# A hybrid of deformable convolution, attention and experts on one core: where the image is added after the sampling, and where TensorE's branch stands

## What is computed

```python
x = x + deform_conv2d(_gn(x), offset_w, offset_b, weight, bias)
x = x + self_attention(_gn(x), ...)            # 1024 x 1024 scores
t = _to_tokens(x)
t = t + attention(_ln_t(t), ...)               # with a fixed bias by distance
t = t + experts(_ln_t(t), ...)                 # top 2 of 8 experts
t = t + linear_attention(_ln_t(t), ...)        # 16 heads of 8
t = t + experts(_ln_t(t), ...)
x = _from_tokens(t, x)
```

## Time and profile before

| | |
|---|---|
| median of three runs | 2330.2 us |
| the profiled execution's own time | 2326.0 us |
| its span, first to last instruction | 2324.2 us |
| TensorE busy, of the span | 81% |
| VectorE busy | 64% |
| ScalarE busy | 45% |
| GpSimd busy | 24% |
| mean granted clock of TensorE | 0.908 of full speed |

### The profile page before, as it was taken

How to read it: one execution, slowest core, us unless ns; L and a number is a source line. 1 busy time by engine, 2 the same in 40 slices (tenths; PEclk the granted TensorE clock), 3 DMA queues, 4 the chain that set the end, 5 groups by cost and what they waited for, 6 DMA issues and landing times.

```text
span 2324.2 us, 35883 instructions
## 1 busy us (share of the span) xinstructions
PE 1879.3 (81%) x10992; PEld 1487.5 (64%) x10992; DVE 1492.3 (64%) x3449; ACT 1039.7 (45%) x1773; POOL 558.3 (24%) x535
## 2 busy tenths in 40 slices
PE   4877869787888878887888878887888878859849
PEld 1655648565766667675766667665767668756736
DVE  2355645767657875678657875677757775685363
ACT  3133317521846245741746345741747326534323
POOL 0000030213231423233230423233140432232130
PEclk7889989987999989998999989998899979979969
DMA  7900674157455946578455956567455945531510
GB/s 260 218 11 18 160 201 123 60 133 195 132 153 155 196 151 174 155 166 204 136 157 150 199 153 174 159 159 188 139 164 148 193 143 161 168 105 58 149 31 10
DMA packets 259912, 337.51 MB, mean 145 GB/s; under 512 B 29552, under 2 KB 191840, under 8 KB 259424
## 3 DMA queue, kind: packets, MB, share of 16 engines
q1 hardware_dynamic: 243648, 297.70, 48.4%
q0 software_dynamic: 14336, 29.39, 4.5%
q10 hardware_dynamic: 1696, 7.66, 0.8%
HBM read 267.56 MB, written 67.08 MB: 144 GB/s over the span
## 4 chain that ended last, share of the span: by engine, by line
PE 33%; issue 19%; DVE 16%; ACT 9%; DMA 6%; DVEq 5%; SPq 5%; POOL 5%; ACTq 3%; POOLq 0%
PE pair L948 5%; PE pair L1067 4%; POOL gotten L808 3%; PE pair L935 3%; ACT L1433 2%; PE pair L861 2%; DVE dist L1642 2%; PE pair L1115 2%; PE pair L1235 2%; PE pair L1160 2%; DMA dist<-hats 2%; PE pair L1225 2%; ACT hidden_sb L1433 2%; ACT L1405 2%; PE pair L881 2%
## 5 line engine op out<-in xcount | busy, mean ns | idle before, releaser
L948 PE MATMUL pair<-dist,thirds 128*128 128x256 f32 (+6 forms) x1440 | 297.5, 358 | 60.6 <-DVE dist L1642 54.2
L948 PEld LDWEIGHTS pair<-dist,thirds 128*128 128x128 f32 x1440 | 257.7, 204 | 110.3 <-DVE dist L1642 57.8
L1067 PE MATMUL pair<-vt,dist 128*128 128x128 f32 x2048 | 269.2, 288 | 32.4 <-DVEq L1745 30.5
L1067 PEld LDWEIGHTS pair<-vt,dist 128*128 128x128 f32 x2048 | 254.8, 202 | 54.4 <-DVEq L1745 47.0
L808 POOL DMA_INDIRECT gotten<-ys,row x224 | 229.4, 1024 | 130.5 <-issue 65.8
L1433 ACT ACTIVATE hidden_sb<-pair,wring 128x128 f32<-128x128 f32 x644 | 184.8, 368 | 157.9 <-PE pair L1115 152.6
L1642 DVE TENSOR_TENSOR dist<-dist,prob 128x1024 f32<-128x1024 f32 x144 | 173.9, 1223 | 90.1 <-DMA prob<-hats 41.8
L1115 PE MATMUL pair<-turned_sb,wring 128*128 128x128 f32 x1288 | 184.4, 287 | 36.2 <-DVEq L1796 17.4
L1115 PEld LDWEIGHTS pair<-turned_sb,wring 128*128 128x128 f32 x1288 | 166.7, 199 | 73.2 <-DVEq L1796 37.5
L796 POOL DMA_INDIRECT xs<-tnB,row x112 | 109.1, 974 | 319.3 <-DVEq L1927 286.8
L1751 DVE TENSOR_REDUCE nmax<-pair 128x1 f32<-128x1024 f32 x128 | 156.6, 1224 | 40.0 <-PE pair L1075 29.3
(11 more groups left out here) (256 smaller groups left out, 3141.9 us busy)
## 6 DMA issues: line engine op xcount, KB each, us to landing
dist<-hats SPq DMA_DIRECT2D x576, 128.0 KB, 4.5
wring<-wa SPq DMA_DIRECT2D x161, 321.0 KB, 3.4
wring<-wb SPq DMA_DIRECT2D x161, 321.0 KB, 3.6
prob<-hats SPq DMA_DIRECT2D x288, 128.0 KB
hats<-dist SPq DMA_DIRECT2D x40, 512.0 KB, 4.0
ys<-by SPq DMA_DIRECT2D x70, 256.0 KB, 2.5
blocks_sb<-xs SPq DMA_DIRECT2D x28, 512.0 KB, 7.0
blocks_sb<-xs SPq DMA_DIRECT2D x14, 448.0 KB, 8.1
```

The source lines that it names most:

```text
L948: last = pe.matmul(pair[0][:, a:b], z[k // 3 % 2][:, c, k % 3, :], rhs(a, b), start=bank not in opened, stop=final, skip_group_check=True)
L1067: last = pe.matmul(psum[bank][:, 0:P], prT[j % 2][:, t, :], vt[:, t, :], start=(t == 0), stop=(t == NT - 1))
```

## The change

It has three parts.

1. *The image is added in the bank.* Ahead of the first half TensorE multiplies `ximg` with the identity matrix into bank "0" (two matmuls of 128x512, `start=True`), so that the halves add to it; `ximg_free` is posted by the second of these. VectorE's xc operation is gone.
2. *Statistics from the bank.* `group_norm` of the second norm takes its statistics from bank "0" itself, first half at once, second half when ScalarE is done with it. ScalarE copies the second half of the bank with the bias into `xc`, waits until VectorE is through the first half's statistics, and copies the first half (semaphores `xc_kept`, `gn1_halves`). The two engines so read different banks at any time. The mean gets the bias by an addition of one column, and the normalization (step 6) waits until both halves of `xc` stand.
3. *TensorE's branch comes earlier.* A half is a function `sampled_half(n)`. Halves 0 to 14 (`LAST_HALVES` = 15) run ahead of the branch, and halves 15, 16 and 17 stand in both arms, first thing.

```diff
+LAST_HALVES = 15
...
                 claim("0")
-                for n in range(HALVES):
+                for h in range(2):
+                    last = pe.matmul(pair[0][:, 512 * h:512 * h + 512], ident, ximg[:, 512 * h:512 * h + 512],
+                                     start=True, stop=False, skip_group_check=True)
+                    opened.add(h)
+                last.then_inc(sem("ximg_free"), 1)
+
+                def sampled_half(n):
                     k, half = divmod(n, 2)
...
-                    if n == HALVES - 1:
-
-                        pe.wait_ge(sem("far_known"), at(m, 1, 1))
...
+                for n in range(LAST_HALVES):
+                    sampled_half(n)
+                pe.wait_ge(sem("far_known"), at(m, 1, 1))
                 flag = pe.value_load(isfar[0:1, 0:1], min_val=0, max_val=1)
+                before_arms = dict(uses)
                 with pe.If(flag > 0):
+                    for n in range(LAST_HALVES, HALVES):
+                        sampled_half(n)
+                    after_arms = dict(uses)
...
                 with pe.Else():
+                    uses.update(before_arms)
+                    for n in range(LAST_HALVES, HALVES):
+                        sampled_half(n)
+                    assert uses == after_arms
                     pe.drain().then_inc(sem("far_used"), len(FAR))
...
+                    act.wait_ge(sem("far_used"), at(m, len(FAR), len(FAR)))
                 with act.Else():
                     act.drain().then_inc(sem("far_z_kept"), UNITS)
+                act.wait_ge(sem("hat_used"), at(m, HALVES, HALVES))
+                act.activation(xc[:, 512:N], psum["0"][:, 512:N], ACT.Identity, bias=const("b0")).then_inc(sem("xc_kept"), 1)
+                act.wait_ge(sem("gn1_halves"), at(m, 1, 1))
+                released(act.activation(xc[:, 0:512], psum["0"][:, 0:512], ACT.Identity, bias=const("b0")), "0")
+                act.drain().then_inc(sem("xc_kept"), 1)
...
                 if step == 0:
+                    from_bank = w == "F"
                     for h in range(2):
-                        dve.bn_stats(bst[:, 6 * h:6 * h + 6], src[:, 512 * h:512 * h + 512])
+                        if from_bank and h:
+                            dve.wait_ge(sem("xc_kept"), at(m, 2, 1))
+                        last = dve.bn_stats(bst[:, 6 * h:6 * h + 6], (psum["0"] if from_bank else src)[:, 512 * h:512 * h + 512])
+                        if from_bank and h == 0:
+                            last.then_inc(sem("gn1_halves"), 1)
...
-                    dve.tensor_copy(gst[:, 0:1], mv[:, 0, 0:1]).then_inc(sem(name + "_stat"), 1)
+                    if from_bank:
+                        dve.tensor_tensor(gst[:, 0:1], mv[:, 0, 0:1], const("b0"), ALU.add).then_inc(sem(name + "_stat"), 1)
+                    else:
+                        dve.tensor_copy(gst[:, 0:1], mv[:, 0, 0:1]).then_inc(sem(name + "_stat"), 1)
...
+                    if w == "F":
+                        dve.wait_ge(sem("xc_kept"), at(m, 2, 2))
                     dve.tensor_scalar(xn, src, rstd[:, 0:1], nmr[:, 0:1], ALU.mult, ALU.add).then_inc(sem(name + "_xn"), 1)
...
                 dve.wait_ge(sem("hat_used"), at(m, HALVES, HALVES))
-                released(dve.scalar_tensor_tensor(xc, psum["0"], const("b0"), ximg, ALU.add, ALU.add), "0")
-                dve.drain().then_inc(sem("ximg_free"), 1)
```

More of the change, by code:

```diff
@@ L1567, in group_norm @@
                     dve.drain()
-                    dve.tensor_tensor(gst[:, 3:4], mv[:, 0, 0:1], gst[:, 2:3], ALU.subtract)
+                    dve.tensor_tensor(gst[:, 3:4], gst[:, 0:1], gst[:, 2:3], ALU.subtract)
                     dve.drain()
```

## The result

| | us |
|---|---|
| before, median of 4 runs | 2328.43 (2320.06 to 2333.60) |
| changed, median of 4 runs | 2350.72 (2346.89 to 2353.26) |
| ratio, 95% interval | 1.0097 (1.0072 to 1.0122) |
| span of the profiled execution, before and changed | 2324.2 and 2349.1 |

The change makes the kernel 22 us slower. The forecast was 2336.0, in a range from 2321 to 2348: the branch was rightly taken for the large term, but its price was wrong.

What follows compares the result with a forecast made beforehand. No engine fills the chain; waits between engines in each of eight images bind. Shorter chain, later branch, low clock and image 6's stall sum to +5.8 us: 2336.0 us against a 2330.2 median, range 2321 to 2348.

Steps and rivals of the forecast that it cites:

- the +5.8 of the sum: All eight images together: 3.6 us less in images 0 to 2, 9.6 more in 3, 4, 5, 7, 0.2 less in 6.
- The branch, images 3 to 7: TensorE's branch ahead of half 15: 4.4 us from flag load to arm, last three halves 2.0 us later per image.
- Images 0 to 2 ... No loss.: In images 0 to 2 the moved branch costs nothing, as hats come slowly; each gains 1.2 us.
- The clock: After TensorE's 2.9 us standstill in images 3 to 7, one half runs at low clock, 1.6 us more.
- The shorter chain: From sampling's end to the second GroupNorm's group product: 2.10 us in place of 3.29, 1.19 less per image.
- The identity products: Two products per image, 0.65 us each, inside TensorE's 1.04 us wait for ScalarE's last chunk: costed at nothing.
- The image load: Next image's load and the expert weights go out early, right after the last hats: nothing gained, nothing lost.
- VectorE's stalls: VectorE's stalls ahead of xc, 3.0 us lost in image 2 and 2.6 in image 6, stay; image 6's covers most delay.
- (A): Rival: TensorE's branch is hidden after all, each image gains 1.2 us, 2320.6 us; chance 0.15.
- (C): Rival: the place doesn't bind, later waits take up what is won or lost, time stays at 2330 us; chance 0.12.
- (B): Rival: low clock lasts over all three halves in images 3 to 7, +21.8 us, 2352.0 us; chance 0.15.
- The two rules of the Trainium skill: A taken branch outside the two pages held must fetch by DMA first; a compare and branch takes about 108 ns.

Runs made afterwards that it cites:

- e8: Not the kernel: 42 taken TensorE branches alone over 4 to 512 products; from 128 products 3.5 to 4.3 us with DMA idle, 6.1 to 6.9 beside loads.
- e1: The changed kernel without its branch move: TensorE's branch back behind all 18 halves; 2326.24 us, ratio 0.999.
- e2: The kernel before with only the branch move: TensorE's flag load and branch ahead of half 15; 2356.30 us, ratio 1.0112.
- e3: The changed kernel with its two arms exchanged: near arm first, entered by falling through, jump behind the last half; 2340.04 us, ratio 1.0055.
- e7: The changed kernel with the far products left out of TensorE's far arm, so the jump is short; 2321.48 us, ratio 0.9979.
- e5: The kernel of e1 with the next image's load let go later, by VectorE between the two statistics and their aggregation; 2321.24 us, ratio 0.9969.
- e4: The changed kernel with the branch ahead of half 10 instead of half 15; 2337.90 us, ratio 1.0053.
- e9: The kernel of e6 with far work cut into pieces, each with its own branch: nine on TensorE, three on VectorE; 2358.14 us, ratio 1.0120.
- e6: The kernel of e5 with the identity products moved from ahead of half 0 to ahead of half 10; 2320.19 us, ratio 0.9964.

## Why the prediction was wrong, point by point

The step that failed is the price of the branch. I took the 4.4 us from the flag's load to the arm out of rows in a quiet place and carried it to places where loads run; on it rest the "No loss" of images 0 to 2 and the delay of images 3 to 7. By the group product the images added 22.3 us, 16.5 more than the +5.8 of the sum: 7.0 of these in images 0 to 2, 4.4 in image 6, and 5.1 in images 3, 4, 5 and 7.

- **The branch, images 3 to 7.** Right in kind, short in size. I took 4.4 us from the flag's load to the arm, out of records of 3.28 to 4.33 us. In image 3 these were measured at a DMA share of 0.03; the new place has 0.71. The hint stood in the rows: the longest record, 4.33, is image 7's, and there the share was 0.79. The branch took 4.20 there, and by the chain of waits the arm came 4.45 us after the transposes' start (826.00 to 830.45) instead of 3.76 (821.74 to 825.5), some 0.7 us more an image.
- **"Images 0 to 2 ... No loss."** This is where the failed step cost most, 7 of the missing 16.5 us. In images 0 and 1 the branch now lies in the midst of the hats' loads: 6.20 and 6.51 us. In image 0 half 15 started at 115.51, not 113.8. In image 1 it started at 323.00, 7.3 us after half 14 and not 4.4, and the granted clock was 0.50 from 322 to 328 us: group product 6.8 us later. e8 shows that other traffic alone makes 4 us into 6 to 7, and the instruction packet's start, 4.0 us into image 1's jump, shows the same here.
- **The clock.** Right in most images: 7.16 - 5.65 = 1.5 us in image 3, forecast 1.6, and much the same in images 4 to 6. In image 7 the block took 8.46 us, so 2.8, for there half 16 ran slow too; in image 1 8.34, a loss that I hadn't counted at all.
- **The shorter chain.** Right: 3.3 to 2.0, so 1.3 us in image 3; forecast 1.19. The statistics out of PSUM take 0.70 us each and follow each other within 0.02.
- **The identity products.** Mis-sized. I priced each of the two at one record, 0.65 us. The group has 32 records for 16 products: each product is two records, 0.59 us each at full clock, and the pair takes 1.88 us (row of L961 at 761.21). In five of the images (1, 3, 4, 5, 7) the first sample came some 0.5 us later against the first chunk than before: 2.5 us. I had costed them at nothing.
- **The image load, "nothing gained, nothing lost".** In the changed kernel I see no loss by it in image 3: the load is issued at 829.79, 0.6 us before the branch is over (830.4). In e1 it was false and cost the whole gain: the load falls on the jump that follows it.
- **VectorE's stalls.** Behind the sampling image 6 did absorb what I forecast: the group product follows the last sample by 2.0 us, where it was 5.9 (1617.24 to 1623.11), so 3.8 as in 2.6 + 1.2. But the image added 4.2 us where I had -0.2, for its sampling also started 5 us late against its first chunk, 0.5 of it the identity products. The granted clock was 0.50 from 1558 to 1564 us, after TensorE had stood still for 2.27 us ahead of the transposes at 1556.66; two groups of chunk products took 2.29 and 2.93 us where others take 1.56. Why the low clock fell there and not elsewhere I have not traced. In image 2 VectorE's stall stayed, and the image gave back 3.7 us of image 1's loss, which I hadn't counted.
- **Rivals.** (A), the hidden branch, is out by e2. (C), absorption, is out: the next image's chunks start as late as the group product came, to within some 1 us. (B)'s time, 2352, came about for another reason, so its closeness to the measured 2350.72 is luck: in image 3 the clock was back by 834 us, about when half 15 had ended, and only in images 1 and 7 was half 16 slow too.
- **The two rules of the Trainium skill.** The rule of a DMA fetch gave the mechanism and held. The 108 ns that the Trainium skill (Advanced Engine Details and Errata, Control Flow Timing) gives for a compare and branch are near the compare that falls through (0.085 us in e3) and half of most short jumps (0.21 in e7); the long ones take 3.3 us and more.

## What to carry to other kernels

A jump over a long arm is a transfer: it costs what the DMA engines let it cost at its new place, so take its duration from a run with the branch at that place, or from rows beside the same loads, and not from quiet rows, and keep loads that nobody needs yet off it. Here the best places were behind the work with the loads held back (e5, 2321 us) and ahead of it with a short arm (e7, 2321, which leaves the far products out). Putting the usual arm first won only half, for the jump then stands behind that arm (e3, 2340), and an earlier branch in a busy stretch did worse than a later one in a quiet one (e4, 2338). A shortened chain gains only up to the next thing on the waiting engine, here the branch, so read what the sequencer holds and not only the releaser that is named.

## What the hardware showed that I had not expected

- From some length on an arm's length no longer matters: 128 and 512 products cost the same jump, 3.5 to 4.3 us with DMA idle and 6.1 to 6.9 beside loads (e8). Beside loads the fetch starts 2.65 us after the jump and then takes as long as without them.
- Nine short jumps over the code of one long one take 6.9 us in place of 3.8 (image 3 of e9 and e6).
- A compare that is not taken costs 0.085 us on TensorE (e3). In image 3 of e4 the taken one was followed by a second stop two records into the arm, 2.54 us, in which one more instruction packet runs (at 808.08).
